# Rows of the later experts gathered by GpSimd without their empty slots, instead of loaded whole by SyncE

## The reference, cut to what matters

```
logits = flat @ Wr + router_bias                    # flat: 2048 tokens x 512
topk_scores, topk_idx = top_k(softmax(logits), 4)   # weights: divided by their sum
pos = place of the token among those of its expert
xb  = zeros(64, 128, 512).at[eid, pos].set(flat[tok], mode='drop')   # CAP = 128
h   = silu(xb @ Wg[e]) * (xb @ Wu[e])
yb  = h @ Wd[e]
out = zeros.at[tok].add(yb[eid, pos] * weight * (pos < 128))
out = out + shared experts(flat)
```

## Time and profile before

| | |
|---|---|
| median of 3 runs | 1113.02 us (1111.92 to 1114.31) |
| profiled execution | 1115.18 us, of which 1113.5 us are the span from the first to the last instruction |
| mean granted clock of TensorE | 0.971 |
| busy share of the span | TensorE 92%, VectorE 65%, GpSimd 53%, ScalarE 45% |
| experts' stage | 838 to 1113 us: last matmul near 1078, then the tables are added up |

### The profile page before, as it was taken

One profiled execution on the slowest core, in us unless ns is written; L12 is line 12 of the kernel. 1 busy time (PEld: TensorE's weight loads), 2 busy tenths in 40 slices (PEclk: granted clock), 3 DMA queues, 4 the chain that ended last, 5 costly groups with the idle time before them and its releaser, 6 DMA issues. The chain is left out here.

```text
span 1113.5 us, 18851 instructions
## 1 busy us (share of the span) xinstructions
PE 1024.4 (92%) x5364; PEld 738.3 (66%) x5364; DVE 722.2 (65%) x1704; ACT 500.2 (45%) x880; POOL 584.8 (53%) x555
## 2 busy tenths in 40 slices
PE   4999999999879999998899999999999999999960
PEld 2555555565437777775389468577778888888850
DVE  3678778777448888886688248167306666667650
ACT  3666656655238888886432211311304333333320
POOL 6566676674326667665524646356432344333551
PEclk9999999999889999999899999999999999999985
DMA  8467655577645332331540241043269999999729
GB/s 268 151 220 249 205 166 179 192 248 283 240 160 167 104 109 104 103 113 67 185 142 18 91 137 48 11 138 112 87 208 333 337 331 308 288 316 336 190 29 194
DMA packets 128254, 199.49 MB, mean 179 GB/s; under 512 B 35975, under 2 KB 44167, under 8 KB 128186
## 3 DMA queue, kind: packets, MB, share of 16 engines
q1 hardware_dynamic: 106394, 160.40, 42.6%
q0 software_dynamic: 21360, 37.48, 13.1%
q10 hardware_dynamic: 432, 0.79, 0.2%
HBM read 133.10 MB, written 87.56 MB: 198 GB/s over the span
## 5 line engine op out<-in xcount | busy, mean ns | idle before, releaser
L957 POOL TENSOR_TENSOR m_down_lo<-wo,m_down_hi 128x512 fp32r<-128x512 f32 x78 | 129.8, 1684 | 76.3 <-ACT m_down_hi L1053 76.3
L566 PE MATMUL bank<-win,vT 128*128 128x512 f32 x256 | 126.6, 609 | 0.0
L734 DVE TENSOR_REDUCE negmax<-bank 128x1 bf16<-128x512 f32 x128 | 85.6, 672 | 43.3 <-PE bank L573 42.9
L659 ACT ACTIVATE win<-bank 128x512 f32<-128x512 f32 x128 | 69.5, 595 | 92.3 <-PE bank L558 89.9
L1067 DVE TENSOR_TENSOR m_up_lo<-w,m_up_hi 128x1024 fp32r<-128x1024 f32 x78 | 95.5, 1226 | 12.4 <-ACT m_up_hi L1025 11.5
L2075 POOL DMA_INDIRECT out<-m_y,m_token x32 | 51.2, 1600 | 87.1 <-DMA out<-m_y,m_token 47.1
L1304 POOL DMA_INDIRECT tab<-stage_up,slot x64 | 65.6, 1025 | 53.3 <-DVE slot L1650 35.4
L2105 PE MATMUL bank<-y,m_w 128*128 128x128 f32 x736 | 89.7, 275 | 0.0
L2219 ACT ACTIVATE sh_gate_a<-bank 128x512 f32<-128x512 f32 (+1 forms) x40 | 20.5, 512 | 151.4 <-PE bank L2212 121.9
L2075 POOL DMA_INDIRECT sums<-m_y,m_token x32 | 50.6, 1581 | 71.7 <-DVE m_y L2169 41.9
L2105 PEld LDWEIGHTS bank<-y,m_w 128*128 128x128 f32 x736 | 86.4, 193 | 0.1
(11 more groups left out here) (302 smaller groups left out, 2492.8 us busy)
## 6 DMA issues: line engine op xcount, KB each, us to landing
tab<-zeros SPq DMA_DIRECT2D x16, 1056.0 KB
m_w<-in_L_ffn_Wg SPq DMA_DIRECT2D x46, 256.0 KB
m_w<-in_L_ffn_Wu SPq DMA_DIRECT2D x46, 256.0 KB
m_w<-in_L_ffn_Wd SPq DMA_DIRECT2D x46, 256.0 KB
m_x<-tab SPq DMA_DIRECT2D x39, 256.0 KB, 2.7
ytab<-m_y SPq DMA_DIRECT2D x39, 256.0 KB, 2.0
stage_up<-tab SPq DMA_DIRECT2D x32, 264.0 KB
m_x<-tab SPq DMA_DIRECT2D x32, 264.0 KB
```

Source lines behind the costliest of these rows:

```text
L566: nc.tensor.matmul(pO[s * 2 + h][:], vT[:, s, sb_, h:h + 2, :].rearrange("p a c -> p (a c)"), probs[:, sb_ % 2, h, :], start=(sb_ == 0), s ...
L659: nc.scalar.activation(probs[:, b % 2, h, :], pS[h][:], ACT.Exp, scale=1.0 / HEAD).then_inc(p_ready, 1)
L734: nc.vector.tensor_reduce(negmax[:, s, m:m + 1], rough_bank(k, m)[:], AX.X, ALU.max, negate=True).then_inc(pm_read, 1)
L957: nc.gpsimd.tensor_tensor(dn_lo[:, m, :], row(wo0, e * MB + m), dn_hi[:, m, :], ALU.subtract).then_inc(dn_lo_ready, 1)
```

## The change

SyncE loads whole rows for the first eight experts alone. For each further expert n, GpSimd gathers its rows from `tab1` by an indirect DMA, with one index per partition; this gather stands in its queue right behind the scatter-add of expert n - 6 (`X_AHEAD`). An index is the slot's row in the table, plus `NO_TOKEN` where the slot is empty, and an index out of bounds moves nothing. Since a skipped slot then still holds what an earlier expert left there, its token's number is replaced by the maximum of it and `empty`, which is 0 or `NO_TOKEN`; so the number is now kept as a float. How many slots of each expert are filled comes from one matmul of ones with the marks `chosen1` at the start of the stage, and two small VectorE operations make the indices of it. TensorE waits for the gather by semaphores of its own, `rows_gathered`, and the transposes of an expert still stand where they stood.

```diff
-            nc.gpsimd.iota(zeros[:, D:D + 1].bitcast(I32), [[0, 1]], base=NO_TOKEN, channel_multiplier=1)
+            nc.gpsimd.iota(zeros[:, D:D + 1], [[0, 1]], base=NO_TOKEN, channel_multiplier=1,
+                           allow_small_or_imprecise_dtypes=True)
...
-                nc.vector.tensor_copy(flat[:, :, D:D + 1].bitcast(I32), tokens[:, g * TPB:g * TPB + TPB].unsqueeze(2))
+                nc.vector.tensor_copy(flat[:, :, D:D + 1], tokens[:, g * TPB:g * TPB + TPB].unsqueeze(2))
...
         def _(sp):
-            for e in range(X_EARLY, X_RING - 1):
+            for e in range(X_EARLY, X_RING):
                 load_rows(sp, T, e)
...
-                e = i + X_RING - 1
-                if e < E1:
-                    need(sp, xT_full, i)
-                    need(sp, y_ready, max(i - 1, min(i, 1)))
-                    load_rows(sp, T, e)
                 e = i + W_RING - 1
...
                     tables[e % SUMS], bass.IndirectOffsetOnAxis(token[:, e % META:e % META + 1], 0), y[:, e % RING, :], None,
                     bounds_check=B * SEQ - 1, oob_is_err=False, compute_op=ALU.add).then_inc(added[e % SUMS], 16)
+                n = e + X_AHEAD
+                if X_RING <= n < E1:
+                    pool.wait_ge(back_read, 1)
+                    nc.gpsimd.indirect_dma_start(
+                        row_slot(T, n % X_RING), None, T["tab1"], bass.IndirectOffsetOnAxis(row_at[:, n:n + 1], 0),
+                        bounds_check=E1 * CAP1 - 1, oob_is_err=False).then_inc(rows_in[n % TPB], 16)
...
         def _(pe):
+            nc.tensor.matmul(pB[1][:, 0:E1], T["onesb"][:], T["chosen1"][:], start=True, stop=True).then_inc(back_full, 1)
...
-                    pe.wait_ge(loaded[e % W_RING], 64 * (e // W_RING + 1))
+                    pe.wait_ge(*weights_of(e))
+                    if e >= X_RING:
+                        pe.wait_ge(rows_in[e % TPB], 32 * B + 16 * ((e - X_RING) // TPB + 1))
...
         def _(dve):
+            dve.wait_ge(back_full, 1)
+            nc.vector.tensor_scalar(empty[:], pB[1][:, 0:E1], T["rowid"][:, 0:1], float(NO_TOKEN), ALU.is_le, ALU.mult)
+            dve.drain()
+            nc.vector.scalar_tensor_tensor(row_at, T["base1"][:], T["rowid"][:, 0:1], empty[:], ALU.add,
+                                           ALU.add).then_inc(back_read, 1)
...
-                    nc.vector.tensor_copy(token[:, m:m + 1], r[:, 0:1].bitcast(I32))
+                    nc.vector.tensor_tensor(token[:, m:m + 1], r[:, 0:1], empty[:, i:i + 1], ALU.max)
```

More of the change, by code:

```diff
@@ L33 @@
 X_EARLY = 4
+X_AHEAD = 6
 XW = D + 16
@@ L157, in build @@
                 T["hidden"] = T["stage_gate"][:].rearrange("p s (n t) -> p (s n) t", t=SEQ)
+                T["gathered"] = [staged.enter_context(nc.semaphore(f"rows_gathered_{j}")) for j in range(TPB)]
                 T["s_w1"] = [staged.enter_context(nc.semaphore(f"m1_loaded_{n}")) for n in range(W_RING)]
@@ L1195, in middle @@
             "mid_small_loaded", "shared_gate_loaded", "shared_back_loaded"))
-        gathered = [sem(f"y0_gathered_{j}") for j in range(TPB)]
+        gathered = T["gathered"]
         beta_ready, wexp_ready = sem("beta_ready"), sem("wexp_ready")
@@ L2005, in experts @@
         match = sb("m1_match", [P, TOP1])
+        empty, row_at = T["chosen1"], T["base1"][:].bitcast(I32)
+        rows_in = T["gathered"]
         xT = T["y0"][:, TPB - 1].rearrange("p k (b t) -> p k b t", b=DB)
@@ L2035, in back_at, with weights_of @@
             return divmod(i - BACK, CHUNKS) if 0 <= i - BACK < (LATE + TPB) * CHUNKS else None
+        def weights_of(e):
+            n = e % W_RING
+            return loaded[n], 48 * (e // W_RING + 1) + (16 if n < X_RING else 0)
         def entries(e):
@@ L2066, in _ @@
                 if e == JOIN:
-                    pool.wait_ge(back_read, LATE)
+                    pool.wait_ge(back_read, LATE + 1)
                     pool.wait_ge(added[e % SUMS], entries(e) - 16)
@@ L2082, in _ @@
                 nc.gpsimd.dma_start(whole[n], part[n], max_dma_last_dim=2 * 4 * D, accum_op=ALU.add).then_inc(joined, 16)
-            pool.wait_ge(back_read, LATE + TPB + 1)
+            pool.wait_ge(back_read, LATE + TPB + 2)
             nc.gpsimd.dma_start(T["out_rows"].rearrange("(t p) d -> p t d", p=P)[:, TILES - TPB:, :], rest[:],
@@ L2110, in _ @@
                         if n == 0:
-                            need(pe, back_read, j - 1)
+                            need(pe, back_read, j)
                         tile = (AT_ONCE + j) % TPB
@@ L2137, in _ @@
                     nc.scalar.activation(g[:, s, :], pH[s][:, 0:CAP1], ACT.Silu).then_inc(g_ready, 1)
-                    act.wait_ge(loaded[i % W_RING], 64 * (i // W_RING + 1))
+                    act.wait_ge(*weights_of(i))
                     need(act, y_full, i - 1)
@@ L2172, in _ @@
                     j = back_at(i - 1)[0]
-                    dve.wait_ge(back_full, j + 1)
+                    dve.wait_ge(back_full, j + 2)
                     if j == 0:
```

## The result

The changed kernel takes 1127.12 us (median of 4 runs, 1126.09 to 1129.65) against 1112.79 of before (median of 4): 1.0127 times as long, 95% interval 1.0110 to 1.0145, some 14 us slower. The profiled execution took 1126.22 us, its span is 1124.5.

A forecast was written before the change was run, and what follows sets the result against it. TensorE, full through the experts' stage, was taken as the bound; start 0.2, join 10.2, clock 2.5 and late gathers 2.0 and 1.0 gave 15.9 us over 1113.0, so 1129 us, range 1124 to 1134 (1120 to 1138 with rivals).

The forecast's parts named there:

- TensorE is the bound, and cheaper DMA gains nothing: Experts' stage: TensorE busy every microsecond from 840 to 1075 us, so cheaper DMA, GpSimd or SyncE can't shorten it.
- The relief of the DMA engines: Experts' stage: gathers skip empty slots, relieving the DMA engines by some 9%; this shortens scatter-adds, not TensorE.
- The start: Before expert 0's transposes: one added matmul and two small VectorE operations, 0.2 us.
- The join: GpSimd's addition of three x_sb tiles to the output delays expert 39's gather; TensorE stalls 10.2 us, bounds 8.3 and 13.0.
- the median row: Earlier trace's gathers of 128 rows: median 5.3 us from issue to landing, taken for expert 39's gather.
- The clock: After the stall at expert 39 TensorE works at half rate for a while: 2.5 us lost, bounds 2.1 and 3.4.
- The row of 4.58 us: Earlier trace: 4.58 us without a matmul, then some 4.3 us of work at half rate, 2.1 us lost.
- Late gathers elsewhere: Gathers behind scatter-adds land late outside the join: 2.0 us before it (bounds 0 and 3.9), 1.0 after (0 and 3).
- gathers that move everything: Case that gathers move empty slots too: no relief, early lateness 3.9 for 2.0, later 3 for 1.0, 1133 us.
- The end: After the last gather, through the last scatter-adds: no change, 0 us, bounds -0.5 and 0.5.
- Sum: Whole kernel: 0.2 + 10.2 + 2.5 + 2.0 + 1.0 = 15.9 us more, giving 1129 us.
- Late throughout: Rival: landings beyond 8.8 us make TensorE wait at each expert, 1138 us; chance 0.20 together with full moves.

The follow-up runs named there:

- e3: Kernel before without SyncE's row loads from expert 8 on and without gathers: ratio to before 1.0000 (0.9982 to 1.0019).
- e9: Changed kernel, distance n - 6 kept, each gather put ahead of the join and of the scatter-add, right behind the wait for y: ratio to before 1.0094.
- e10: Changed kernel with each gather behind the scatter-add of expert n - 7 instead of n - 6: ratio to before 1.0083 (1.0059 to 1.0107).
- e4: Changed kernel with indices that skip nothing, so each gather moves all 128 rows: ratio to before 1.0149 (1.0122 to 1.0177).
- e8: Changed kernel with each gather behind the scatter-add of expert n - 5 instead of n - 6: ratio to before 1.0571 (1.0535 to 1.0606).

## Why the prediction was right, point by point

- **TensorE is the bound, and cheaper DMA gains nothing.** Right, and shown by e3: all row traffic gone, the same time within 2 us.
- **The relief of the DMA engines.** Predicted 9% of their time; from 845 to 1087 us the two queues took 89.2% of it before (67.0 and 22.2) and 81.3% after (51.3 and 30.0), 8 less. Right.
- **The start**, 0.2 us: from TensorE's first work in the stage to the start of y(0) it is 8.12 us before (837.60 to 845.72) and 8.16 after (834.09 to 842.25). It cost less than 0.1.
- **The join.** The mechanism was right to the expert: T(39), held by g(39) behind s(33) behind the join. Its size was off: 7.9 us instead of 10.2, and below the lower bound of 8.3. Two parts of the sum did it. The join was issued 1.25 us earlier in the stage (968.83 against 971.19, while the stage was only 1.11 ahead at y(36)), since s(31) landed earlier; the prediction had set the relief off against g(38) and called both 0. So g(39) was issued 0.8 us sooner. And its rows were there within 4.0 us, not 5.3: together 2.1 less. Full gathers took 4.4 us in e9 and 5.9 in e10. The Trainium skill's figure (DMA: Bandwidth & Descriptors, Anatomy of one DMA), an estimated 3.6 with the issue, was nearer to the 4.0 of this gather than the median row was, and further from the 5.9 of e10.
- **The clock.** Predicted 2.5; what is left of the step of 9.7 us beside the wait of 7.9 is 1.8. T(39) began at 986.56, and the granted clock was low in 988 to 992 for about half of the stretch (0.78), so some 3 us of work at half rate. The row of 4.58 us would have said 2.1.
- **Late gathers elsewhere.** Ahead of the join 2.4, predicted 2.0; behind it 2.5, predicted 1.0 and within its bound of 3. Only about half of it stands as waits in the profile, as said above. e9 shows that what stands ahead in the queue makes them late: with the same distance of 6, but the gather ahead of its scatter-add, 0.3 is left of the 2.4, and 0.3 behind the join. The prediction's 3.9 for gathers that move everything has its like in e4, with 4.0.
- **The end**, 0: from TensorE's last matmul to the end of the span it is 35.0 us after, 35.5 before. Right.
- **Sum.** Measured 9.7 + 2.4 + 2.5 = 14.6 against the predicted 15.9; the join's part was 3.0 too high (12.7), the others 1.7 too low (3.2, with the start). The two errors partly cancel, and that the total came within 2 us of 1127.12 is in part luck; that the join carries most of the loss is not.
- **Late throughout** didn't come at n - 6, but e8 shows it one expert further on, and shows that its working was wrong. The prediction took T(n) to y(n), 13.3 us, and a loop of 6 experts. The loop that binds is T(n), y(n - 2), s(n - 2), g(n + 4): four experts. At the edge both give the same landing, 8.8 us, but beyond it each microsecond costs an expert a fourth and not a sixth, and at n - 5 a third. That error is a good part of why 9 to 18 us, plus the join, were expected for e8 where 63 came. With a loop of three experts and the same landings of 6 to 7 us the estimate would have been 0.33 to 0.66 us for each of 55 experts, 18 to 37. The rest is that landings were longer in e8, 7.8 us from s(19) to T(24), and the half clock.

## What to carry to other kernels

A gather put into an engine's queue behind something that waits inherits that wait: look for the longest stall of that queue, count how far ahead of use the gather is issued, and compare. Here the join held s(33) back by 10.9 us (from 969.7, 0.84 behind y(33), to 980.57), and g(39) had 2.9 to spare: 8 us of wait. With the gathers two experts earlier no wait for rows was left in the profile. For a lead in a pipelined loop, find which stage of which item releases it: the engine's order can make the loop shorter than the ring, and then one expert less of distance costs much more than one would think, here 63 us in place of 14. And traffic taken off full DMA engines was worth nothing here, since the compute engine beside them never waited.

## What the runs showed of the hardware that was not expected

- A gather by GpSimd took 1.07 us of issue in the median for 128 rows of 2,112 B, with skipping and without, where 0.95 was taken from the earlier trace rows. A gather's packet holds two rows, and a skipped pair remains a packet: 13,520 packets with skipping and 13,469 without, at 14.30 and 22.82 MB.
- From its issue to the first use of its rows a full gather took 4.0, 4.4 and 5.9 us, with a DMA share of 0.66, 0.76 and 0.84 over that time.
- In each of the waits of TensorE of 4.8, 6.8, 7.2, 7.3, 7.9 and 8.9 us in these runs the granted clock fell to the half rate before work began again; of the 22 shorter ones of e8 (0.4 to 2.8 us) four brought it.
